# A two-layer graph network on one core: stores moved behind loads, GpSimd's order changed, part of V's split moved to GpSimd

## The chip, the cores and the metric

One NeuronCore of a Trainium2 chip runs the whole program. The metric is device time in microseconds of that core; each kernel was run several times, and the median is the number that counts. A separate profiled execution gives the trace.

## What is computed

64 graphs of 256 nodes with 512 features each go through two layers. `x` is (64, 256, 512), `adj` is (64, 256, 256), all float32.

```python
# layer 0
h = relu(layernorm(x))
q, k, v = h @ Wq.T + bq, h @ Wk.T + bk, h @ Wv.T + bv
weight = adj * exp(q @ k.T)
x = x + (weight / weight.sum(axis=2)) @ v
# layer 1
h = relu(layernorm(x))
A_hat = adj + eye
d = A_hat.sum(-1) ** -0.5
x = x + (A_hat * d[:, None] * d[None, :]) @ (h @ W + b)
```

## The kernel before

Every matrix product is done in float32 accuracy with three passes over "high" and "low" parts: a tile X is split into X_hi (rounded, written mostly by ScalarE, ACT) and X_lo = X - X_hi (a subtraction on VectorE, DVE, or GpSimd, POOL). TensorE (PE) then multiplies hi by hi, hi by lo and lo by hi (`product`, L1158, L1160 and L1161). Two products are done by a scheme with seven block products instead of eight: V = h Wv (`values`, blocks V1 to V7), and Y = Z W of layer 1 (`part`, R1 to R7). The sums that the scheme needs are `ht_sum` (POOL, L338 to L343) and `z_sum` (DVE, L858 to L869).

The program is a software pipeline over graphs: `steps` calls `step(this, ...)` for each graph, as a loop over 3 to 62 and with separate steps at either end. One step does layer 0 of graph `this`, layer 1 of graph `this - 1`, and prepares graphs `this + 1` and `this + 2`. There is no planner. Each engine has its own `step` with its order written out by hand, and semaphores are all that ties engines together. An engine works its list strictly in order, so a waiting instruction holds back all behind it.

What follows is one step in the order in which PE walks it, with the helpers of the other engines that matter below.

- **G** = M applied to ht (48 matmuls): ACT's `g_high` (L513) and DVE's `g_low` (L764) split it, for j = 0 and j = 1.
- **V** (42 matmuls): V1, V6, V5, V4, V2, V7, V3. V6 wants both halves of `ht_sum_lo` (POOL L349). V2 wants `v_p1` (ACT `keep_p1`, L498). V7 wants `v_u2` (DVE `value_u2`, L773).
- **Z** of the graph before (24 matmuls): wants `h1_lo` (DVE L883) and `hat_lo` (POOL L368).
- **S**, the attention logits (24 matmuls), then R1, and R2 behind `z_lo[1]` (DVE L862), then R4 and R5 behind the exponentials `e` (ACT L660).
- **O** = P V (24 matmuls), which wants all of `v_lo` and `p_lo`, with R6 between its halves, then R7 and R3.

The scale of layer 1's normalization runs through three engines: DVE computes `neg_mean_1` (L937), ACT the squares (L544), DVE `ve_1` (L1028), POOL the power `rs_1` (L406), DVE `sc_1` and `nb_1` (L1033, L1035, semaphore `ln_1_ready`), then ACT writes `h1` and `h1_hi` (L598, L600), and DVE `h1_low` (L883) and `add_bias` (L878, into x1b).

DVE's `turn_dn` (L849) waits for POOL's `row_norms` (L323, L325). `transpose_adjacency` (L841) overwrites `adjt` and so waits for POOL's `hat_low` (L368), which reads it. `sums_of_l` (L944 twice, then L949) comes between `z_low_first` and `z_low_second` (L862).

V's split has three pieces: `v_hi[0]`, `v_hi[1]`, `v_hi[2]` on ACT (L616, L625, L652), and their low parts on DVE: `value_low` (L794), `value_low_upper` (L801) and `value_low_lower` (L806, 128x512). POOL computes ht_sums, rs_x (L319), z_sum_lo (L393) and ht_lo (L455) in this order at the end of its step, and at the start diagonal_ones (L361), ht_sums_low (L349 twice), row_norms, rs_1, hat_low, x_with_bias (L330, twice).

All loads and stores go through SyncE's one queue (SP), issued in this order in a step: h to a scratch in DRAM (L259), the two stores of y behind `y_ready` (L265), adj_in (L269), the four loads of h_blocks (L205), xb (L249), x_in (L243), the two small stores of dn (L284), dn_row (L288), adj_blocks (L199).

Of the kernel before, what the change touches and what calls it, by code (L numbers as in the profile page):

```python
# [12 lines left out]
def gnn_program(nc, x, adj, wq, bq, wk, bk, wv, bv, w, b, out):  # L13
# [19 lines left out]
    with ctx:  # L33
# [57 lines left out]
        with nc.sbuf_tensor("v", [P, NT, 2, HD + 2], fp32) as v:  # L91
# [79 lines left out]
        vk_ready = sems("vk_ready")  # L171
        g_done, g_hi_ready, g_lo_ready = sems("g_done"), sems("g_hi_ready"), sems("g_lo_ready")
        v_done, v_hi_ready, v_lo_ready = sems("v_done", 7), sems("v_hi_ready", 3), sems("v_lo_ready", 3)
        v_p1_ready, v_p5_ready, v_u2_ready, v_u3_ready = (
            sem("v_p1_ready"), sem("v_p5_ready"), sem("v_u2_ready"), sem("v_u3_ready"))
        v12_ready, v21_ready, v22_ready = sem("v12_ready"), sem("v21_ready"), sem("v22_ready")
# [49 lines left out]
        @block.sync  # L226
        def _(sp):
            for o in range(DC):
                sp.dma_start(wk_in[:, o, :], wk[o * P:(o + 1) * P, :]).then_inc(wqk_loaded[o], 16)
            sp.dma_start(x_in[:], x[0].rearrange("(t p) d -> p t d", p=P)).then_inc(x_loaded, 16)  # L230
            sp.dma_start(wv_in[:], wv.rearrange("(c p) d -> p c d", p=P)).then_inc(wv_loaded, 16)
            sp.dma_start(adj_in[:], adj[0].rearrange("(t p) n -> p t n", p=P)).then_inc(adj_loaded, 16)
            sp.dma_start(xb[:], x[0].rearrange("(t p) d -> p t d", p=P)).then_inc(xb_loaded, 16)
            load_blocks(sp, adj.rearrange("g n m -> (g n m)")[0:N * N])
            for block, (i, j) in zip((B11, T3, B21, B22), ((0, 0), (0, 1), (1, 0), (1, 1))):
                sp.dma_start(w_parts[:, block], w.rearrange("(i c p) (j d) -> i j p c d", i=2, c=2, j=2)[i, j]).then_inc(
                    w_loaded, 16)

            adj_flat, x_flat = adj.rearrange("g n m -> (g n m)"), x.rearrange("g n d -> (g n d)")

            def load_x(this):
                x_second = x_flat[bass.ds(sp.snap((this + 1) * (N * D)), N * D)]
                sp.dma_start(x_in[:], x_second.rearrange("(t p d) -> p t d", p=P, d=D)).then_inc(x_loaded, 16)  # L243

            def load_xb(this):
                x_this = x_flat[bass.ds(sp.snap((this - 1) * (N * D)), N * D)]
                sp.wait_ge(x1_ready[0], this - 1)
                sp.wait_ge(x1_ready[1], this - 1)
                sp.dma_start(xb[:], x_this.rearrange("(t p d) -> p t d", p=P, d=D)).then_inc(xb_loaded, 16)  # L249

            def step(this, prev, main, ahead, older=True, second=True):
                if prev and not older:
                    load_xb(this)
                if prev and ahead:
                    sp.wait_ge(h_ready[0], this + 1)
                    sp.wait_ge(h_ready[1], this + 1)
                    if older:
                        sp.wait_ge(h_blocks_loaded, (this - 2) * (16 * P // 32))
                    sp.dma_start(h_dram.rearrange("(t p) d -> p t d", p=P), h[:]).then_inc(h_stored, 16)  # L259
                    if not older:  # L260
                        load_x(this)
                if prev and older:
                    for t in range(NT):
                        sp.wait_ge(y_ready[t], this - 2)
                        sp.dma_start(out[this - 3, t * P:(t + 1) * P, :], y[:, t, :]).then_inc(stored, 16)  # L265
                if main and ahead:
                    adj_next = adj_flat[bass.ds(sp.snap(this * (N * N)), N * N)]
                    sp.wait_ge(rsum_ready, this)
                    sp.dma_start(adj_in[:], adj_next.rearrange("(t p n) -> p t n", p=P, n=N)).then_inc(adj_loaded, 16)  # L269
                if prev and ahead:  # L270
                    sp.wait_ge(h_stored, (this - 1) * 16)
                    if older:
                        sp.wait_ge(ht_ready[1], this)
                    load_h_blocks(sp)
                if main and prev and older:
                    load_xb(this)
                if second and prev and older:
                    load_x(this)
                if main:
                    sp.wait_ge(dn_turned_ready, this)  # L280
                    if prev:
                        sp.wait_ge(dn_row_loaded, (this - 1) * 16)
                    for t in range(NT):
                        sp.dma_start(dn_dram[t], dn_turned[t::32, :]).then_inc(dn_stored, 16)  # L284
                    sp.wait_ge(dn_stored, this * (16 * NT))
                    if prev:
                        sp.wait_ge(s_sum_ready, this - 1)
                    sp.dma_start(dn_row[:], dn_dram.rearrange("t q c -> (t q c)").partition_broadcast(P)).then_inc(  # L288
                        dn_row_loaded, 16)
                if main and ahead:  # L290
                    sp.wait_ge(adjt_ready, this)
                    load_blocks(sp, adj_next)
                if second and not prev:
                    sp.wait_ge(h_ready[0], this + 1)
                    sp.wait_ge(h_ready[1], this + 1)
                    load_x(this)

            steps(sp, step)
            for t, a, ready, value in ((0, 0, y11_ready, B), (0, 1, y_ready[0], B), (1, 0, y_ready[1], B),
                                       (1, 1, y_ready[1], B + 1)):  # L300
                sp.wait_ge(ready, value)
                cols = slice(a * HD, (a + 1) * HD)
                sp.dma_start(out[B - 1, t * P:(t + 1) * P, cols], y[:, t, cols]).then_inc(stored, 16)
            sp.wait_ge(stored, B * 16 * NT + 16 * NT)

        @block.gpsimd
        def _(pool):
# [80 lines left out]

            def z_sums_low_second(graph, this=None):
                if this is not None:  # L390
                    pool.wait_ge(v_lo_ready[2], this)
                pool.wait_ge(z_sum_hi_ready, 2 * graph)
                pool.tensor_tensor(z_sum_lo[:, S3:S4 + 1], z_sum[:, S3:S4 + 1], z_sum_hi[:, S3:S4 + 1].bitcast(fp32),  # L393
                                   ALU.subtract).then_inc(z_sum_lo_by_pool, 1)

            def step(this, prev, main, ahead, older=True, second=True):
                if prev and older:

                    diagonal_ones(this - 1)
                    if main:  # L400
                        ht_sums_low(this)
                        pool.wait_ge(d_ready, this - 1)
                        pool.wait_ge(dn_turned_ready, this - 1)
                        row_norms(this)
                        pool.wait_ge(ve_1_done, this - 1)
                        pool.tensor_tensor(rs_1[:], ve_1[:], minus_half[:], ALU.pow).then_inc(rs_1_done, 1)  # L406
                    hat_low(this - 1, older)
                if prev and not older:
                    ht_sums_low_half(this, 0)
# [35 lines left out]
                if main and ahead:  # L445
                    pool.wait_ge(v_done[V3], this)
                    ht_sums(this + 1)
                if second and main and (older or not prev):
                    x_power(this + 2)
                if main and prev and older:  # L450
# [11 lines left out]
        def _(act):  # L462
# [113 lines left out]
            def step(this, prev, main, ahead, older=True, second=True):  # L576
# [12 lines left out]
                    x1_squares(this)  # L589
                if main and not prev:  # L590
                    act.wait_ge(u_ready, 1)
                if main and (not prev or older):
                    g_high(0, this)
                if prev:

                    for t in range(NT):
# [4 lines left out]
                                       bias=nb_1[:, t:t + 1]).then_inc(h1_ready[t], 1)  # L601
                        if main and not older and t == 0:
                            keep_p1(this)
                if main:
                    if not prev or older:
                        keep_p1(this)
# [81 lines left out]
        def _(dve):  # L688
# [287 lines left out]
            def step(this, prev, main, ahead, older=True, second=True):  # L976
# [45 lines left out]
                if prev and main and older:  # L1022
# [5 lines left out]
                    dve.tensor_scalar(ve_1[:], x1_square[:], 1.0 / D, EPS, ALU.mult, ALU.add).then_inc(ve_1_done, 1)  # L1028
                    dve.wait_ge(d_ready, this - 1)
                    dve.wait_ge(neg_mean_1_ready, this - 2)  # L1030
                    turn_dn(this, prev)
                    dve.wait_ge(rs_1_done, this - 1)
                    dve.tensor_tensor(sc_1[:], rs_1[:], d[:], ALU.mult).then_inc(sc_1_done, 1)  # L1033
                    dve.wait_ge(sc_1_done, this - 1)
                    dve.tensor_tensor(nb_1[:], neg_mean_1[:], sc_1[:], ALU.mult).then_inc(ln_1_ready, 1)  # L1035
                    transpose_adjacency(this, prev)
                    g_low(0, this)
                    h1_low(0, this - 1)
                    add_bias(0, this - 1)
                    value_u2(this)  # L1040
                    h1_low(1, this - 1)
                if main and not prev:
                    value_u2(this)
                    x_variance(this + 1)
# [45 lines left out]
                if main:  # L1090
# [11 lines left out]
                    p_low(this)  # L1102
                    if prev and older:
                        value_low_upper(this)
                        value_low_lower(this)
                        if second:
                            x_shift(this + 2)
                    if prev and not older:
# [43 lines left out]
        def _(pe):  # L1152
# [173 lines left out]
            def step(this, prev, main, ahead, older=True, second=True):  # L1326
# [61 lines left out]
                if main:  # L1388

                    pe.wait_ge(p_lo_ready[1], this)  # L1390
                    if not prev:
                        pe.wait_ge(consts_ready, 2)
                    for lower_part in v_lo_ready:
                        pe.wait_ge(lower_part, this)
                    pe.wait_ge(v12_ready, this)
                    pe.wait_ge(v21_ready, this)
                    pe.wait_ge(vk_ready[1], this)
# [39 lines left out]
```

## Time and profile before

| | us |
|---|---|
| median of 3 runs | 1873.71 |
| lowest, highest | 1871.33, 1873.95 |
| the profiled execution, its own time | 1872.89 |
| its span, first to last instruction | 1871.1 |

Busy shares of the span: PE 90%, DVE 85%, ACT 66%, POOL 57%; the granted TensorE clock averages 0.974 of full speed, and the DMA engines are busy 44% of the time on the main queue. A step of the loop takes some 28 us. A row of a timeline reads: start in us, duration in us, engine, line, operation, output<-inputs, shapes, count, and in brackets how long the engine had been idle before it and what released it. Consecutive DVE or ACT instructions overlap by some 0.07 us in such rows, since the records hold the start and the end of an instruction that is pipelined with the next.

### The profile page before, as it was taken

How to read it: one execution, taken by the hardware profiler on the slowest of the kernel's cores; microseconds unless marked ns; L12 is line 12 of the kernel's file. 1: busy time of each engine (PE TensorE's matmuls, PEld its weight loads, DVE VectorE, ACT ScalarE, POOL GpSimd, SP SyncE). 2: the span in 40 equal slices, each digit the busy share in tenths (PEclk: the TensorE clock that was granted, in tenths of full speed). 3: DMA queues.
4: the chain of work that ended last, by engine and by line, in shares of the span. 5: the costliest groups of instructions: out<-in, count | busy, mean ns of one | idle time of the engine just before them, and what ended most of it. 6: DMA issues, size and time to landing. Idle time of an engine off the chain costs nothing. (4 is left out here: it accounts for less than half of the span.)

```text
span 1871.1 us, 42042 instructions
## 1 busy us (share of the span) xinstructions
PE 1677.5 (90%) x13201; PEld 1623.8 (87%) x13201; DVE 1590.6 (85%) x3894; ACT 1240.0 (66%) x2890; POOL 1058.6 (57%) x1165
## 2 busy tenths in 40 slices
PE   8799899898898898999998988988988988988987
PEld 7788889898898898888888988988988988988987
DVE  7888888888888888888888888888888888888887
ACT  5566666766766666676676666666666666666663
POOL 4555655565556456556555555555555555564562
PEclk9899998999999999999999999999999999999998
DMA  5344353454453443543544544544544544534421
GB/s 172 84 117 125 96 129 104 111 133 107 107 131 104 114 126 95 129 117 104 129 111 110 129 110 112 129 111 111 129 108 113 128 107 105 133 101 117 132 69 48
DMA packets 495265, 212.68 MB, mean 114 GB/s; under 512 B 402576, under 2 KB 428688, under 8 KB 495248
## 3 DMA queue, kind: packets, MB, share of 16 engines
q1 hardware_dynamic: 493328, 210.89, 44.4%
q10 hardware_dynamic: 1920, 1.58, 0.3%
q8 instruction: 9, 0.15, 0.0%
q14 instruction: 8, 0.07, 0.0%
HBM read 146.28 MB, written 66.13 MB: 114 GB/s over the span
## 5 line engine op out<-in xcount | busy, mean ns | idle before, releaser
L330 POOL TENSOR_TENSOR xb<-xb,bv_row 128x512 f32<-128x512 f32 x128 | 163.7, 1300 | 406.5 <-DMA xb<-in_x_dram 392.6
L1158 PE MATMUL ps<-ht_hi,m_hi 128*128 128x256 f32 x1024 | 286.2, 279 | 2.8 <-issue 2.7
L1160 PE MATMUL ps<-ht_lo,m_hi 128*128 128x256 f32 x1024 | 288.4, 282 | 0.0
L1161 PE MATMUL ps<-ht_hi,m_lo 128*128 128x256 f32 x1024 | 287.5, 281 | 0.0
L1158 PE MATMUL ps<-w_hi,z_hi 128*128 128x256 f32 x384 | 125.4, 327 | 115.4 <-DVE z_lo L862 59.3
L898 DVE SCALAR_TENSOR_TENSOR late<-ps,d,late 128x256 f32<-128x256 f32 x504 | 219.5, 476 | 4.5 <-PE ps L1161 2.1
L1158 PE MATMUL ps<-v_hi,p_hi 128*128 128x258 f32 (+1 forms) x512 | 155.7, 304 | 64.1 <-DVE v_lo L801 54.6
L1158 PEld LDWEIGHTS ps<-w_hi,z_hi 128*128 128x128 f32 x384 | 75.1, 195 | 141.3 <-DVE z_lo L862 72.5
L1158 PEld LDWEIGHTS ps<-ht_hi,m_hi 128*128 128x128 f32 x1024 | 193.4, 189 | 3.2 <-issue 2.9
L529 ACT ACTIVATE unused_x<-x_in 128x512 f32<-128x512 f32 x128 | 79.7, 624 | 172.5 <-DMA x_in<-in_x_dram 172.5
L1161 PEld LDWEIGHTS ps<-ht_hi,m_lo 128*128 128x128 f32 x1024 | 193.5, 189 | 0.0
L1160 PEld LDWEIGHTS ps<-ht_lo,m_hi 128*128 128x128 f32 x1024 | 193.2, 189 | 0.0
L393 POOL TENSOR_TENSOR z_sum_lo<-z_sum,z_sum_hi 128x512 fp32r<-128x512 f32 x64 | 82.6, 1290 | 172.1 <-DVE v_lo L806 156.0
L1158 PEld LDWEIGHTS ps<-v_hi,p_hi 128*128 128x128 f32 x512 | 101.8, 199 | 76.5 <-issue 70.2
L349 POOL TENSOR_TENSOR ht_sum_lo<-ht_sum,ht_sum_hi 128x512 fp32r<-128x512 f32 x128 | 164.2, 1305 | 2.5 <-ACT ht_sum_hi L508 2.5
L598 ACT ACTIVATE late<-late,nb,sc 128x512 f32<-128x512 f32 x128 | 103.6, 809 | 89.5 <-DVE nb L1035 86.2
L455 POOL TENSOR_TENSOR ht_lo<-ht,ht_hi 128x512 fp32r<-128x512 f32 x124 | 158.3, 1300 | 0.0
L1158 PE MATMUL ps<-w_hi,z_sum_hi 128*128 128x256 f32 x512 | 149.9, 293 | 5.6 <-DVE late L898 4.9
L319 POOL TENSOR_TENSOR rs_x<-ve_x,minus_half 128x2 f32<-128x2 f32 x64 | 51.3, 801 | 180.4 <-DVE ve_x L815 180.4
L1160 PE MATMUL ps<-w_lo,z_sum_hi 128*128 128x256 f32 x512 | 149.3, 292 | 0.0
L1160 PE MATMUL ps<-v_lo,p_hi 128*128 128x258 f32 (+1 forms) x512 | 149.2, 291 | 0.0
L1161 PE MATMUL ps<-w_hi,z_sum_lo 128*128 128x256 f32 x512 | 148.8, 291 | 0.0
(195 smaller groups left out, 7051.9 us busy)
## 6 DMA issues: line engine op xcount, KB each, us to landing
x_in<-in_x_dram SPq DMA_DIRECT2D x64, 512.0 KB, 4.9
xb<-in_x_dram SPq DMA_DIRECT2D x64, 512.0 KB, 4.4
out_dram<-late SPq DMA_DIRECT2D x126, 256.0 KB, 2.2
h_scratch<-h SPq DMA_DIRECT2D x62, 512.0 KB, 2.8
h_blocks<-h_scratch SPq DMA_DIRECT2D x248, 128.0 KB, 3.9
adj_in<-in_adj_dram SPq DMA_DIRECT2D x64, 256.0 KB, 3.1
adj_blocks<-in_adj_dram SPq DMA_DIRECT2D x256, 64.0 KB, 2.5
dn_row<-dn_scratch SPq DMA_DIRECT2D x64, 128.0 KB, 2.9
```

Of the source, the lines that this page charges most:

```text
L319: pool.tensor_tensor(rs_x[:], ve_x[:], minus_half[:], ALU.pow).then_inc(rs_x_done, 1)
L330: last = pool.tensor_tensor(xb[:, t, :], xb[:, t, :], bv_row[:], ALU.add)
L349: pool.tensor_tensor(ht_sum_lo[:, pair], ht_sum[:, pair], ht_sum_hi[:, pair].bitcast(fp32), ALU.subtract).then_inc(ht_sum_lo_ready, 1)
L393: pool.tensor_tensor(z_sum_lo[:, S3:S4 + 1], z_sum[:, S3:S4 + 1], z_sum_hi[:, S3:S4 + 1].bitcast(fp32), ALU.subtract).then_inc(z_sum_lo_by ...
L455: pool.tensor_tensor(ht_lo[:, 2 * j:2 * j + 2, :], ht[:, 2 * j:2 * j + 2, :], ht_hi[:, 2 * j:2 * j + 2, :].bitcast(fp32), ALU.subtract).th ...
L529: last = act.activation(unused_x[:, t, :], x_in[:, t, :], ACT.Copy, accum_out=x_sum[:, t:t + 1])
L598: act.activation(h1[:, t, :], x1[:, t, :], ACT.Relu, scale=sc_1[:, t:t + 1], bias=nb_1[:, t:t + 1])
L898: return dve.scalar_tensor_tensor(y[:, t, cols], ps[:, bank, 0:HD], scale[:, t:t + 1], base[:, t, cols], ALU.mult, ALU.add)
L1158: pe.matmul(dst, a_hi[:, c, cols], b_hi[:, c, :], start=(first and c == 0), stop=False, skip_group_check=not first)
L1160: pe.matmul(dst, a_hi[:, c, cols], b_lo[:, c, :], start=False, stop=False, skip_group_check=not first)
L1161: end = pe.matmul(dst, a_lo[:, c, cols], b_hi[:, c, :], start=False, stop=(c == chunks - 1), skip_group_check=not first)
```

## The change

Five things are done.

- SyncE issues the two stores of y behind the loads of xb and x_in instead of ahead of adj_in.
- GpSimd writes only the first half of ht_sum_lo before rs_1, then waits for `ln_1_ready` (a wait that no data asks for), and then writes the second half and does row_norms.
- GpSimd writes the low part of V's lower rows (128x512) behind ht_sums, under a semaphore of its own, and its z_sum_lo waits for v_lo_ready[1] in place of v_lo_ready[2]. VectorE no longer does value_low_lower in the loop's steps.
- ScalarE writes h1 and h1_hi for both halves ahead of g_high(0).
- VectorE does h1_low(0) and add_bias(0) directly after nb_1, then turn_dn, transpose_adjacency, h1_low(1), g_low(0) and value_u2.

```diff
@@ -171,6 +171,7 @@
         vk_ready = sems("vk_ready")
         g_done, g_hi_ready, g_lo_ready = sems("g_done"), sems("g_hi_ready"), sems("g_lo_ready")
         v_done, v_hi_ready, v_lo_ready = sems("v_done", 7), sems("v_hi_ready", 3), sems("v_lo_ready", 3)
+        v_lo_by_pool = sem("v_lo_by_pool")
         v_p1_ready, v_p5_ready, v_u2_ready, v_u3_ready = (
             sem("v_p1_ready"), sem("v_p5_ready"), sem("v_u2_ready"), sem("v_u3_ready"))
         v12_ready, v21_ready, v22_ready = sem("v12_ready"), sem("v21_ready"), sem("v22_ready")
@@ -259,10 +260,6 @@
                     sp.dma_start(h_dram.rearrange("(t p) d -> p t d", p=P), h[:]).then_inc(h_stored, 16)
                     if not older:
                         load_x(this)
-                if prev and older:
-                    for t in range(NT):
-                        sp.wait_ge(y_ready[t], this - 2)
-                        sp.dma_start(out[this - 3, t * P:(t + 1) * P, :], y[:, t, :]).then_inc(stored, 16)
                 if main and ahead:
                     adj_next = adj_flat[bass.ds(sp.snap(this * (N * N)), N * N)]
                     sp.wait_ge(rsum_ready, this)
@@ -276,6 +273,10 @@
                     load_xb(this)
                 if second and prev and older:
                     load_x(this)
+                if prev and older:
+                    for t in range(NT):
+                        sp.wait_ge(y_ready[t], this - 2)
+                        sp.dma_start(out[this - 3, t * P:(t + 1) * P, :], y[:, t, :]).then_inc(stored, 16)
                 if main:
                     sp.wait_ge(dn_turned_ready, this)
                     if prev:
@@ -388,7 +389,7 @@
 
             def z_sums_low_second(graph, this=None):
                 if this is not None:
-                    pool.wait_ge(v_lo_ready[2], this)
+                    pool.wait_ge(v_lo_ready[1], this)
                 pool.wait_ge(z_sum_hi_ready, 2 * graph)
                 pool.tensor_tensor(z_sum_lo[:, S3:S4 + 1], z_sum[:, S3:S4 + 1], z_sum_hi[:, S3:S4 + 1].bitcast(fp32),
                                    ALU.subtract).then_inc(z_sum_lo_by_pool, 1)
@@ -398,12 +399,14 @@
 
                     diagonal_ones(this - 1)
                     if main:
-                        ht_sums_low(this)
+                        ht_sums_low_half(this, 0)
+                        pool.wait_ge(ve_1_done, this - 1)
+                        pool.tensor_tensor(rs_1[:], ve_1[:], minus_half[:], ALU.pow).then_inc(rs_1_done, 1)
+                        pool.wait_ge(ln_1_ready, this - 1)
+                        ht_sums_low_half(this, 1)
                         pool.wait_ge(d_ready, this - 1)
                         pool.wait_ge(dn_turned_ready, this - 1)
                         row_norms(this)
-                        pool.wait_ge(ve_1_done, this - 1)
-                        pool.tensor_tensor(rs_1[:], ve_1[:], minus_half[:], ALU.pow).then_inc(rs_1_done, 1)
                     hat_low(this - 1, older)
                 if prev and not older:
                     ht_sums_low_half(this, 0)
@@ -445,6 +448,10 @@
                 if main and ahead:
                     pool.wait_ge(v_done[V3], this)
                     ht_sums(this + 1)
+                if main and prev and older:
+                    pool.wait_ge(v_hi_ready[2], this)
+                    pool.tensor_tensor(v_lo[:, 1, :, 0:HD], v[:, 1, :, 0:HD], v_hi[:, 1, :, 0:HD].bitcast(fp32),
+                                       ALU.subtract).then_inc(v_lo_by_pool, 1)
                 if second and main and (older or not prev):
                     x_power(this + 2)
                 if main and prev and older:
@@ -589,7 +596,7 @@
                     x1_squares(this)
                 if main and not prev:
                     act.wait_ge(u_ready, 1)
-                if main and (not prev or older):
+                if main and not prev:
                     g_high(0, this)
                 if prev:
 
@@ -601,6 +608,8 @@
                                        bias=nb_1[:, t:t + 1]).then_inc(h1_ready[t], 1)
                         if main and not older and t == 0:
                             keep_p1(this)
+                    if main and older:
+                        g_high(0, this)
                 if main:
                     if not prev or older:
                         keep_p1(this)
@@ -1028,17 +1037,17 @@
                     dve.tensor_scalar(ve_1[:], x1_square[:], 1.0 / D, EPS, ALU.mult, ALU.add).then_inc(ve_1_done, 1)
                     dve.wait_ge(d_ready, this - 1)
                     dve.wait_ge(neg_mean_1_ready, this - 2)
-                    turn_dn(this, prev)
                     dve.wait_ge(rs_1_done, this - 1)
                     dve.tensor_tensor(sc_1[:], rs_1[:], d[:], ALU.mult).then_inc(sc_1_done, 1)
                     dve.wait_ge(sc_1_done, this - 1)
                     dve.tensor_tensor(nb_1[:], neg_mean_1[:], sc_1[:], ALU.mult).then_inc(ln_1_ready, 1)
-                    transpose_adjacency(this, prev)
-                    g_low(0, this)
                     h1_low(0, this - 1)
                     add_bias(0, this - 1)
+                    turn_dn(this, prev)
+                    transpose_adjacency(this, prev)
+                    h1_low(1, this - 1)
+                    g_low(0, this)
                     value_u2(this)
-                    h1_low(1, this - 1)
                 if main and not prev:
                     value_u2(this)
                     x_variance(this + 1)
@@ -1102,7 +1111,6 @@
                     p_low(this)
                     if prev and older:
                         value_low_upper(this)
-                        value_low_lower(this)
                         if second:
                             x_shift(this + 2)
                     if prev and not older:
@@ -1390,8 +1398,12 @@
                     pe.wait_ge(p_lo_ready[1], this)
                     if not prev:
                         pe.wait_ge(consts_ready, 2)
-                    for lower_part in v_lo_ready:
-                        pe.wait_ge(lower_part, this)
+                    pe.wait_ge(v_lo_ready[0], this)
+                    pe.wait_ge(v_lo_ready[1], this)
+                    if prev and older:
+                        pe.wait_ge(v_lo_by_pool, this - 2)
+                    else:
+                        pe.wait_ge(v_lo_ready[2], this)
                     pe.wait_ge(v12_ready, this)
                     pe.wait_ge(v21_ready, this)
                     pe.wait_ge(vk_ready[1], this)
```

## Rows read from the trace of the kernel before

**Rows 1.** The waits of the whole trace: engine, line waited for, total us, times, longest

```profile
POOL xb L330 <- DMA xb<-in_x_dram: 392.6, 60, 7.7
PE ps L1158 <- DVE z_lo L862: 59.3, 59, 1.8
```

**Rows 2.** Timeline of VectorE in one step of the loop, up to the scale

```profile
1191.45 0.42 DVE L801 TENSOR_TENSOR v_lo<-v,v_hi 128x256 fp32r<-128x256 f32 x1
1191.79 0.69 DVE L806 TENSOR_TENSOR v_lo<-v,v_hi 128x512 fp32r<-128x512 f32 x1
...
1196.66 0.17 DVE L927 RECIPROCAL rinv<-ps 128x1 f32<-128x1 f32 x1 [0.70 <-PE ps L1161]
...
1197.72 0.82 DVE L937 TENSOR_SCALAR neg_mean<-x_sum 128x2 f32<-128x2 f32 x1
...
1200.13 0.17 DVE L1028 TENSOR_SCALAR ve<-x_square 128x2 f32<-128x2 f32 x1
...
1201.75 1.25 DVE L1033 TENSOR_TENSOR sc<-rs,d 128x2 f32<-128x2 f32 x1 [0.25 <-POOL rs L406]
1203.03 0.16 DVE L1035 TENSOR_TENSOR nb<-neg_mean,sc 128x2 f32<-128x2 f32 x1
```

**Rows 3.** The same timeline, from transpose_adjacency to the next step's L801

```profile
1203.22 0.71 DVE L841 STREAM_TRANSPOSE adjt<-adj_blocks 128x512 f32<-128x512 f32 x1
...
1206.54 0.43 DVE L773 TENSOR_TENSOR v_u<-ps,v_p 128x258 f32<-128x258 f32 x1 [0.40 <-ACT v_p L498]
1206.88 0.68 DVE L883 TENSOR_TENSOR h_lo<-late,h_hi 128x512 fp32r<-128x512 f32 x1
1207.48 0.74 DVE L878 SCALAR_TENSOR_TENSOR late<-b_row,sd,late 128x512 f32<-128x512 f32 x1
1208.14 0.87 DVE L764 SCALAR_TENSOR_TENSOR g_lo<-ps,u_col,g_hi 128x256 fp32r<-128x256 f32 x2
...
1212.53 0.24 DVE L811 TENSOR_SCALAR neg_mean<-x_sum 128x2 f32<-128x2 f32 x1
...
1214.35 0.95 DVE L944 CUSTOM_DVE_ANT_0 unused_a<-adj_kept,dn_row,dn_wide 128x256 f32<-128x256 f32 x1
...
1215.42 0.68 DVE L862 TENSOR_TENSOR z_lo<-ps,z_hi 128x512 fp32r<-128x512 f32 x1
...
1219.52 0.42 DVE L801 TENSOR_TENSOR v_lo<-v,v_hi 128x256 fp32r<-128x256 f32 x1
```

**Rows 4.** Timeline of GpSimd in the same step

```profile
1197.22 2.56 POOL L349 TENSOR_TENSOR ht_sum_lo<-ht_sum,ht_sum_hi 128x512 fp32r<-128x512 f32 x2
...
1201.02 0.69 POOL L406 TENSOR_TENSOR rs<-ve,minus_half 128x2 f32<-128x2 f32 x1
1201.67 1.30 POOL L368 TENSOR_TENSOR hat_lo<-adjt,hat_hi 128x512 fp32r<-128x512 f32 x1
1209.31 2.55 POOL L330 TENSOR_TENSOR xb<-xb,bv_row 128x512 f32<-128x512 f32 x2 [6.33 <-DMA xb<-in_x_dram]
...
1214.21 0.81 POOL L343 TENSOR_TENSOR ht_sum<-ht,ht_sum 128x256 f32<-128x256 f32 x1
```

**Rows 5.** Timelines of ScalarE, SyncE's queue and TensorE in the same step

```profile
1203.95 0.80 ACT L600 ACTIVATE h_hi<-late,nb,sc 128x512 fp32r<-128x512 f32 x1
...
1214.00 0.62 ACT L652 ACTIVATE v_hi<-v 128x512 fp32r<-128x512 f32 x1
...
1205.03 0.44 SPq L249 DMA_DIRECT2D xb<-in_x_dram  x1
...
1192.79 0.36 PE L1158 MATMUL ps<-v_hi,p_hi 128*128 128x258 f32 x1 [1.22 <-DVE v_lo L801]
...
1207.31 0.28 PE L1158 MATMUL ps<-wt_hi,ht_sum_hi 128*128 128x256 f32 x1
```

**Rows 6.** L944 and L1035 in the whole trace: ns min/median/max, first and last start

```profile
L944 DVE CUSTOM_DVE_ANT_0 unused_a<-adj_kept,dn_row,dn_wide x128: 470/918/1504, 50.5 to 1836.1; 128x256 f32<-128x256 f32 x128
...
L1035 DVE TENSOR_TENSOR nb<-neg_mean,sc x62: 160/161/164, 96.8 to 1826.6; 128x2 f32<-128x2 f32 x62
```

## The prediction

> **What bounds the kernel now.** I read the waits first, then one step of the loop on each engine. TensorE looks like the bound at 90% busy, but its waits end on VectorE: it waits for z_lo once in nearly every step [rows 1]. The longest wait of the trace is GpSimd's for xb, 6.54 us a step (392.6 over 60) [rows 1]. That wait is the first thing to follow, since the stores of y stand ahead of that load.
>
> I take the step that starts with L801 at 1191.45 and count from there; the next L801 comes at 1219.52, so it is 28.07 long [rows 2, 3]. VectorE is nearly always at work in it, and four of its instructions are longer than their size explains. L1033 handles 128x2 elements in 1.25 us where L1035, of the same kind and size, takes 0.16. It ends at 1203.00, just after GpSimd's hat_low ends (1202.97) [rows 2, 4]. L937, also 128x2, takes 0.82 and ends when the first half of L349 must be ending [rows 2, 4]. The second L944 takes 0.95 where the shortest takes 0.47, and it ends 0.28 after GpSimd's L343 (1215.02) [rows 3, 4, 6]. So certain VectorE instructions stand still until GpSimd's running instruction is over. Those seen here read two tiles in SBUF, or are tiny ones. The transposes and the reads of PSUM show nothing of it.
>
> This makes the late xb load costly although GpSimd is only 57% busy: load, x_with_bias, ht_sums, then the second L944, then z_lo, then TensorE. L343's end is 5.71 behind L330's start, and L862 starts 0.40 behind that [rows 3, 4].
>
> The Trainium skill (SBUF, "Who interferes with whom") states this as a lock: a VectorE instruction with two SBUF inputs contends with a GpSimd instruction that reads SBUF, and whichever is first holds the pair to its end. L1033 agrees with 1.25 against 0.16 [rows 2].
>
> **Part 1, the stores behind the loads.** This removes SyncE's wait for y from in front of adj_in, h_blocks, xb and x_in. xb was issued at 1205.03 and used at 1209.31 [rows 4, 5]. Without the wait the order is free to go as soon as h has been stored, some us earlier, so GpSimd will wait for the other condition of x_with_bias, the end of add_bias(1) on VectorE, which in this step would be 1208.22 (L878 starts at 1207.48 and lasts 0.74) [rows 3]. GpSimd could start 1.05 earlier. The stores themselves cost nothing where they land: y is not overwritten until the next step's R1. The dn stores come behind them on the queue, but no longer behind the x loads' data.
>
> **Part 2, value_low_lower to GpSimd.** VectorE loses L806, 0.69 [rows 2]. TensorE's O started at 1.34, 0.31 after L806's end at 1.03 [rows 2, 5]. Now it can start some 0.37 after L801's end at 0.42 (one more wait to pass, 0.06 as an estimate), so 0.79: **0.55 gained**. All that follows O moves: the second L927 from 5.21 to 4.66. GpSimd's z_sum_lo, and with it everything up to the first half of ht_sum_lo, comes 0.61 earlier (L801's end instead of L806's).
>
> **Part 3, around the scale.** L937 ended at 7.09 with the first half of L349; 0.61 earlier is 6.48. The squares and ve_1 follow at the same distance: ve_1 ends at 8.24 instead of 8.85 [rows 2]. GpSimd is idle then, so rs_1 (0.69) runs at once, to 8.96, and then waits, which leaves L1033 free: 0.16. With L1035's 0.16 and 0.04 between each, nb is done at 9.36. It was 11.74: **2.4 us earlier** [rows 2, 4].
>
> But VectorE's next work is now h1_low(0), which waits for ScalarE's h1 and h1_hi. L600 ended 1.56 after nb's end (1204.75 against 1203.19) [rows 2, 5], so h1_low(0) starts at 10.95. Before, transpose_adjacency and g_low(0) covered this. Here VectorE stands idle for 1.6 us. From the starts in rows 3, h1_low takes 0.60 to the next instruction and add_bias 0.66. They end at 12.2. Meanwhile GpSimd, released at 9.4, does half of L349 (1.28), row_norms (about 0.9) and hat_low (1.30): 12.9 at best. Its row_norms and hat_low read SBUF, as h1_low and add_bias do, and meet them between 10.95 and 12.2. At worst hat_low starts only at 12.25 and ends at 13.55. I take the worst, since both VectorE instructions read two SBUF tiles and stand back to back. transpose_adjacency waits for hat_low: 13.58. Then 0.64 for it (as between 1203.22 and g_low at 1203.86), h1_low(1) 0.60, g_low(0) 0.79, value_u2 0.34, add_bias(1) 0.66. g_low(1) starts at **16.61; it was 16.69** [rows 3]. So the 2.4 us are given back almost whole, to waits for ScalarE and GpSimd. Bounds: 15.9 if hat_low isn't delayed, 17.3 if row_norms is pushed behind add_bias(0) and hat_low comes yet 0.65 later.
>
> value_u2 ends at 16.05. TensorE, 0.55 earlier than before, would reach V7 at 15.3 (15.86 less 0.55 [rows 5]) and waits 0.75. That is covered: with 60 matmuls of 0.12 from V7 to the end of S and six more for R1, it reaches R2 near 24.0, while z_lo (below) comes later. If z_lo came at 23.3 the cover would be gone, and it would cost up to 0.1.
>
> **Part 4, what the shorter wait for xb buys.** GpSimd starts x_with_bias at 16.75 (it was 17.86) and by the same 5.71 ends ht_sums at 22.46. On VectorE, L811 came 4.39 after g_low(1), of which 0.28 was L790 standing behind GpSimd; I take 4.11, so 20.72, with its end at 21.0. The first L944 follows 0.77 later, at 21.8, when L343 has just begun (21.65). It stands until 22.4, the second one takes 0.47 more: both are done at 23.1.
>
> **Part 5, the new instruction on GpSimd.** v_lo's lower rows wait for ScalarE's L652. That ended 1.85 after L811's end (1214.62 against 1212.77) [rows 3, 5]: now 22.85. So GpSimd is ready with its 1.3 us instruction (L368 has the same size, 1.30 [rows 4]) at 22.9, and gets its turn when the second L944 is over, near 23.05. VectorE's next is sd (L949), 128x2, from two SBUF tiles, ready at 23.15: 0.2 too late. It would stand as L1033 did, until 24.3. L862 starts at **24.35; it was 23.97**. The instruction that left VectorE (0.69) comes back as a wait of up to 1.2, at the place on which TensorE waits.
>
> The Trainium skill (Perfetto Trace Analysis, "Optimizing Scalar/DVE Operations") warns that moving work between VectorE and GpSimd might not help because of their common read port. By that alone the 0.55 of part 2 would be returned; the sum above goes by the rows.
>
> **The sum.** From L862 to the next L801 was 4.10 and is unchanged: the step is 28.45. The average step before was 28.36 (L1035's first and last start, 61 steps [rows 6]), longer than the one shown by 0.29: 0.21 by a later xb (6.54 against 6.33), which goes away, and 0.08 by disturbed steps, which stay. So 28.53 against 28.36, 0.17 more, times 62 steps: +10.5. On the profiled execution's 1872.89 that is 1883.4. The median of the runs is 0.8 higher: **1884 us**.
>
> **The rivals.**
>
> A. sd slips in ahead of v_lo. Then L862 starts at 23.25, the step is 27.43 on average, 0.93 less, 62 times: -58, **1816 us**. Against it: my 0.2 us margin. For it: that margin is the difference of two sums of six terms, each good to 0.1. It decides at L944's end: if ht_sums ends 0.3 earlier relative to VectorE, or ScalarE's L652 comes 0.25 later, sd is first. Since GpSimd no longer waits for a transfer, all steps should fall the same way. Chance 0.32.
>
> B. The waits behind h1 are longer: row_norms and hat_low queue behind VectorE's pair and g_low(1) starts at 17.3. That is 0.7 on top of the forecast: +43, **1927 us**. Chance 0.07.
>
> C. The forecast's mechanism, sized differently. 0.3 us a step is 19 us. With g_low(1) at 16.3 the result is 1865. The chance of the case is 0.61, of which 0.16 fall below, 0.11 within and 0.34 above the bounds of 0.2% that a measurement of this kernel can tell from no change.
>
> D. The change doesn't do what it says: xb stays late, because the queue is held by the store of h rather than by y. Then L862 can't come before the old 23.97. Included in C, as it gives no more than that.
>
> **How the numbers follow.** Faster: 0.32 of A and 0.16 of C, 0.48. Same: 0.11. Slower: 0.34 and 0.07, 0.41. The forecast is 1884, its own range 1862 to 1902. Faster and slower both hold much, so the whole range takes in A with an error of 10 us: 1806 to 1902, leaving out B and the tails.
>
> **What would show it.** GpSimd's wait for xb should be released by add_bias (L878), not by the DMA. L1033 should take 0.16. VectorE should show a new idle time of 1.6 us before h1_low(0), released by h_hi, and one before transpose_adjacency, released by hat_lo. TensorE should wait for v_u before V7. L949 decides: a median near 1.2 us is the forecast, 0.16 is rival A. If L944 takes 0.47 both times, my timing of ht_sums against VectorE is wrong, and the time will lie below 1816.

## The result

The changed kernel is slower by 0.3%: a median of 1879.03 us (1877.07 to 1880.03, 7 runs) against 1873.71 us (7 runs), a ratio of 1.0031 with a 95% interval of 1.0018 to 1.0044. Its profiled execution has a span of 1877.3 us.

VectorE's busy time fell from 1590.6 us to 1502.2, by 88 us, GpSimd's rose from 1058.6 to 1176.3, and the whole got 5 us longer. The lines of the page of the changed kernel (first the busy times, and from the chain of work that ended last its shares by engine):

```profile
PE 1680.4 (90%) x13201; PEld 1623.4 (86%) x13201; DVE 1502.2 (80%) x3832; ACT 1231.7 (66%) x2890; POOL 1176.3 (63%) x1227
...
DVE 36%; POOL 32%; issue 22%; ACT 5%; PE 1%; DVEq 1%; POOLq 1%; SPq 1%; DMA 0%; ACTq 0%
```

The waits of the changed kernel answer to [rows 1]. The 392.6 us behind the DMA are gone, and GpSimd waits for add_bias (L887 is the old L878). TensorE has a new wait for value_u2 (L782), and VectorE has three: for h1_hi, for hat_lo, and a longer one for rs.

```profile
POOL xb L331 <- DVE late L887: 205.4, 62, 3.3
...
DVE h_lo L892 <- ACT h_hi L607: 100.2, 63, 1.6
...
DVE adjt L850 <- POOL hat_lo L369: 63.3, 62, 1.1
...
DVE sc L1041 <- POOL rs L404: 56.5, 62, 0.9
...
PE ps L1166 <- DVE v_u L782: 51.9, 62, 1.1
PE ps L1166 <- DVE z_lo L871: 46.7, 61, 0.8
```

One step of the changed kernel on VectorE, from L810 (the old L801) at 1167.48 to the next at 1195.94. It is 28.46 us long, and every time below is to be read less 1167.48 against [rows 2, 3]. The last row is of the next step and answers to L1033:

```profile
1178.61 0.69 DVE L892 TENSOR_TENSOR h_lo<-late,h_hi 128x512 fp32r<-128x512 f32 x1 [1.59 <-ACT h_hi L607]
...
1181.20 0.71 DVE L850 STREAM_TRANSPOSE adjt<-adj_blocks 128x512 f32<-128x512 f32 x1 [1.01 <-POOL hat_lo L369]
...
1184.18 0.87 DVE L773 SCALAR_TENSOR_TENSOR g_lo<-ps,u_col,g_hi 128x256 fp32r<-128x256 f32 x2
...
1189.33 1.02 DVE L953 CUSTOM_DVE_ANT_0 unused_a<-adj_kept,dn_row,dn_wide 128x256 f32<-128x256 f32 x1
...
1190.28 0.48 DVE L953 CUSTOM_DVE_ANT_0 unused_a<-adj_kept,dn_row,dn_wide 128x256 f32<-128x256 f32 x1
...
1190.80 1.13 DVE L958 TENSOR_TENSOR sd<-s_sum,dn_wide 128x2 f32<-128x2 f32 x1
1191.85 0.68 DVE L871 TENSOR_TENSOR z_lo<-ps,z_hi 128x512 fp32r<-128x512 f32 x1
...
1195.94 0.42 DVE L810 TENSOR_TENSOR v_lo<-v,v_hi 128x256 fp32r<-128x256 f32 x1
...
1205.11 0.16 DVE L1041 TENSOR_TENSOR sc<-rs,d 128x2 f32<-128x2 f32 x1 [0.91 <-POOL rs L404]
```

GpSimd in the same step, answering to [rows 4]:

```profile
1178.63 1.22 POOL L326 TENSOR_TENSOR dn_wide<-rsum,minus_half 128x2 f32<-128x2 f32 x1
1179.81 1.30 POOL L369 TENSOR_TENSOR hat_lo<-adjt,hat_hi 128x512 fp32r<-128x512 f32 x1
1184.43 2.54 POOL L331 TENSOR_TENSOR xb<-xb,bv_row 128x512 f32<-128x512 f32 x2 [3.32 <-DVE late L887]
...
1189.32 0.74 POOL L344 TENSOR_TENSOR ht_sum<-ht,ht_sum 128x256 f32<-128x256 f32 x1
1190.51 1.40 POOL L453 TENSOR_TENSOR v_lo<-v,v_hi 128x512 fp32r<-128x512 f32 x1 [0.44 <-ACT v_hi L661]
```

L453 starts at 1190.51, L958 at 1190.80. L453 ends at 1191.91, L958 at 1191.93, with 1.13 us for 256 numbers that take 0.16 elsewhere. Then L871 starts, on which TensorE waits. The collision is in nearly every step, as the line of L958 over the whole trace shows (ns min/median/max):

```profile
L958 DVE TENSOR_TENSOR sd<-s_sum,dn_wide x64: 160/1130/1133, 52.5 to 1843.7; 128x2 f32<-128x2 f32 x64
...
L1043 DVE TENSOR_TENSOR nb<-neg_mean,sc x62: 160/161/164, 95.3 to 1831.4; 128x2 f32<-128x2 f32 x62
```

L1043 gives the average step: (1831.4 - 95.3) / 61 = 28.46, against 28.36 before. From one start of L1043 to the next, all 61 steps lie between 28.44 and 28.60 us. In the kernel before they lie between 27.46 and 30.38 (starts of L1035).

The granted clock is a rival for the cause, since its mean is only 0.976 here. In 17 places of the loop, from 455 us on in every third step, TensorE runs at half clock (1.2 GHz instead of 2.4) for some 3.4 us. Such a stretch and one without, one step on (length, busy us, then the granted clock, DMA share and GB/s):

```profile
1222.50:1226.50 4.00, 3.65 (x18) 0.59 0.00 0
1251.00:1255.00 4.00, 3.19 (x24) 1.00 0.00 0
```

The first two steps that hold such a stretch take 28.60 and 28.51 us, and the 15 later ones are as long as the steps without, so the half clock costs the changed kernel next to nothing.

### The profile page after: what moved, and what is told of

It reads as the page before. It is cut to its first block, busy times and chain, and to the rows that moved or that the text cites. A ratio compares the mean times of both kernels' runs of the same rounds, so it can differ in the third digit from the quotient of the medians.

```text
span 1877.3 us, 42042 instructions
## 1 busy us (share of the span) xinstructions
PE 1680.4 (90%) x13201; PEld 1623.4 (86%) x13201; DVE 1502.2 (80%) x3832; ACT 1231.7 (66%) x2890; POOL 1176.3 (63%) x1227
## 4 chain that ended last, share of the span: by engine, by line
DVE 36%; POOL 32%; issue 22%; ACT 5%; PE 1%; DVEq 1%; POOLq 1%; SPq 1%; DMA 0%; ACTq 0%
POOL ht_sum_lo L350 8%; POOL ht_lo L462 8%; DVE g_lo L773 5%; DVE unused_a L953 4%; POOL hat_lo L369 4%; DVE ht L841 4%; POOL dn_wide L326 4%; POOL adjt L362 3%; POOL rs L404 2%; DVE z_lo L871 2%; DVE late L887 2%; ACT z_sum_hi L577 2%; ACT e L669 1%; DVE z_sum L876 1%; DVE p_lo L982 1%
## 5 line engine op out<-in xcount | busy, mean ns | idle before, releaser
L1166 PE MATMUL ps<-wt_hi,ht_sum_hi 128*128 128x256 f32 (+1 forms) x512 | 151.1, 295 | 52.5 <-DVE v_u L782 51.9
L892 DVE TENSOR_TENSOR h_lo<-late,h_hi 128x512 fp32r<-128x512 f32 x128 | 85.9, 671 | 100.2 <-ACT h_hi L607 100.2
L634 ACT ACTIVATE v_hi<-v 128x256 fp32r<-128x256 f32 x64 | 26.8, 419 | 199.1 <-DVE v L797 199.1
L577 ACT ACTIVATE z_sum_hi<-z_sum 128x512 fp32r<-128x512 f32 x128 | 79.9, 625 | 116.3 <-DVE z_sum L876 116.3
L1166 PEld LDWEIGHTS ps<-wt_hi,ht_sum_hi 128*128 128x128 f32 x512 | 96.2, 188 | 65.7 <-DVE v_u L782 64.8
```

Source lines behind the costliest of these rows:

```text
L577: act.activation(z_sum_hi[:, pair], z_sum[:, pair], ACT.Copy).then_inc(z_sum_hi_ready, 1)
L892: dve.tensor_tensor(h1_lo[:, t, :], h1[:, t, :], h1_hi[:, t, :].bitcast(fp32), ALU.subtract).then_inc(h1_lo_ready[t], 1)
L1166: pe.matmul(dst, a_hi[:, c, cols], b_hi[:, c, :], start=(first and c == 0), stop=False, skip_group_check=not first)
```

## The experiments

The theory under test: VectorE's instructions with two SBUF inputs stand behind a running GpSimd instruction, so what counts is when GpSimd's instructions fall against them, not how busy either engine is. The rivals: the step is set by VectorE's busy time, by TensorE's new wait, or by none of these. All ratios are to the kernel before on the same chip. Those chips differ by up to 0.5% in the kernel before (1873.71 us for the result, 1865.25 and 1872.02 in the two groups of runs below), so ratios are compared, not times. Where no row is shown, the time at which something starts in a step is the median over the kernel's steps, counted from the start of L801 or the line that answers to it.

| kernel | parts in it | us | ratio, 95% interval |
|---|---|---|---|
| p1_stores | stores behind loads | 1820.26 | 0.9760 (0.9737 to 0.9783) |
| p2_vlow | V's lower rows on GpSimd | 1886.77 | 1.0128 (1.0095 to 1.0161) |
| p3_scale | order around the scale | 1866.20 | 0.9996 (0.9979 to 1.0013) |
| e1_sd_first | all three, sd kept ahead | 1819.68 | 0.9753 (0.9729 to 0.9777) |
| p1_p2 | first two | 1849.94 | 0.9881 (0.9862 to 0.9901) |
| p1_p3 | first and third | 1858.04 | 0.9927 (0.9908 to 0.9946) |
| p1_p2_sd | first two, sd kept ahead | 1782.14 | 0.9525 (0.9506 to 0.9544) |
| p1_p2_sd_scale2 | the same and another order of the scale | 1720.99 | 0.9195 (0.9176 to 0.9214) |

### sd kept ahead of GpSimd's new instruction

```diff
                 if main and prev and older:
                     pool.wait_ge(v_hi_ready[2], this)
+                    pool.wait_ge(sd_ready, this)
                     pool.tensor_tensor(v_lo[:, 1, :, 0:HD], ...
```

> The changed kernel with one wait more: GpSimd's low part of V's lower rows also waits for sd_ready, so that VectorE's sd (128x2) is always issued ahead of it. Theory one, sd stands behind GpSimd's 1.3 us instruction and that delays z_lo and TensorE: sd falls from a median of 1.13 us to 0.16, the second part of z_lo starts near 23.4 us after L810 instead of 24.4, the step falls from 28.46 to 27.5 us, 62 steps, and the time to some 1818 us. Theory two, the step is set elsewhere (by V7's wait for value_u2 on TensorE, or by VectorE's own new idle time): sd is short, another wait takes up most of the gain, and the time stays above 1860 us.

Measured: 0.9753. One more wait makes the changed kernel 2.8% faster (0.9753 / 1.0031 = 0.972). sd has a median of 160 ns:

```profile
L959 DVE TENSOR_TENSOR sd<-s_sum,dn_wide x64: 160/160/573, 53.3 to 1785.7; 128x2 f32<-128x2 f32 x64
...
L1044 DVE TENSOR_TENSOR nb<-neg_mean,sc x62: 160/161/164, 96.1 to 1773.4; 128x2 f32<-128x2 f32 x62
```

The step is (1773.4 - 96.1) / 61 = 27.50 us, as expected under theory one. TensorE still waits for value_u2, and for longer (66.0 us instead of 51.9), without holding the time at 1860. The stretches at half clock are gone from the loop too (the mean is 0.992), but they had cost nothing. That settles the cause: 0.96 us a step were lost to this one collision.

### The stores alone

```diff
-                if prev and older:
-                    (the two stores of y, behind y_ready)
                 if main and ahead:
 ...
                 if second and prev and older:
                     load_x(this)
+                if prev and older:
+                    (the two stores of y, behind y_ready)
```

> The kernel before with the stores of y moved behind the loads, and nothing else. Theory one, the late load of xb shifts GpSimd's sums against VectorE and so sets z_lo: x_with_bias starts with the end of add_bias instead of with the DMA, L862 starts at 23.4 after L801 instead of 24.0 to 24.1, and the time is 1873.7 less 62 times 0.8, some 1825 us. Theory two, GpSimd at 57% busy is off the path and the load is hidden anyway: the wait moves from the DMA to another releaser and the time stays within 5 us of 1873.7.

Measured: 0.9760, 1820.26 us. The stores moved behind the loads are worth 2.4% by themselves, although GpSimd is 58% busy and no VectorE instruction was removed. In a step that starts with L801 at 1130.31 (the next is at 1157.79, 27.48 later), the end of the two L944 no longer hangs on a late load:

```profile
1153.10 0.47 DVE L944 CUSTOM_DVE_ANT_0 unused_a<-adj_kept,dn_row,dn_wide 128x256 f32<-128x256 f32 x1
...
1153.62 0.16 DVE L949 TENSOR_TENSOR sd<-s_sum,dn_wide 128x2 f32<-128x2 f32 x1
1153.70 0.69 DVE L862 TENSOR_TENSOR z_lo<-ps,z_hi 128x512 fp32r<-128x512 f32 x1
...
1157.79 0.42 DVE L801 TENSOR_TENSOR v_lo<-v,v_hi 128x256 fp32r<-128x256 f32 x1
```

L862 is at 23.39. It was 23.97 in the step of [rows 3]. The average step falls by more, from 28.36 to 27.48, since that step was one of the shorter ones: with no load waited for, all steps take 27.47 to 27.50, the last two apart. TensorE's wait for it fell from 59.3 us [rows 1] to 14.6, and GpSimd's for xb is released by add_bias:

```profile
POOL xb L330 <- DVE late L878: 335.0, 62, 5.4
...
PE ps L1158 <- DVE z_lo L862: 14.6, 60, 0.3
```

### V's lower rows on GpSimd alone

The diff is the third bullet of the change with TensorE's wait for it: L806 leaves VectorE, the GpSimd instruction comes in behind ht_sums.

> The kernel before with the low part of V's lower rows moved to GpSimd, and nothing else. Theory one: O starts 0.55 us earlier, but GpSimd's new instruction stands directly behind the sums, is ready before sd and makes sd wait some 1.2 us; L862 starts near 24.6 after L801 instead of 24.0, the step is 0.5 to 0.7 us longer and the time some 1905 to 1915 us. Theory two, VectorE's busy time is what counts: 0.69 us off VectorE gives 0.55 us a step back, some 1840 us.

Measured: 1.0128. Moving 0.69 us of work off the busier engine makes the kernel 1.3% slower. VectorE's busy time didn't even fall in the trace (1601.2 us against 1590.6), since standing still counts as busy. sd's duration:

```profile
L954 DVE TENSOR_TENSOR sd<-s_sum,dn_wide x64: 163/1102/1249, 53.0 to 1847.7; 128x2 f32<-128x2 f32 x64
```

The mechanism is theory one's; the size was expected at 1905 to 1915 us, and it is 1887, on a chip where the kernel before takes 1865. So 22 us were lost where 31 to 41 were expected. The load of xb came earlier too, which the expectation left out: the stores of y are issued 0.59 us earlier in the step than in the kernel before, and x_with_bias starts at 17.24 instead of 18.04. That this is all of the difference isn't shown.

### The order around the scale alone

> The kernel before with the order around x1's scale alone (GpSimd, ScalarE and VectorE). Theory one: L1033 falls from 1.24 to 0.16 us, and the gain goes into a wait for h1_hi of 1.6 us and one for hat_lo of about 1 us on VectorE, so that g_low(1) starts 0.4 to 0.5 us later than before; the late xb hides that as GpSimd's sums are later still, and the time stays within 10 us of 1873.7. Theory two: the shorter scale is worth its 1.1 us a step, some 1806 us.

Measured: 0.9996. sc takes 0.16 us here instead of 1.24, and nothing comes of it, as theory one has it. g_low(1) starts at 17.30 instead of 16.69, and the second part of z_lo, still set by the late xb, at 24.06 instead of 24.16. VectorE waits 100.2 us for h1_hi and 63.7 us for hat_lo:

```profile
DVE h_lo L887 <- ACT h_hi L602: 100.2, 63, 1.6
...
DVE adjt L845 <- POOL hat_lo L368: 63.7, 62, 1.1
```

### Two parts at a time

The first expectation is for p1_p2, the second for p1_p3.

> The stores behind the loads and V's lower rows on GpSimd, with the scale's order as in the kernel before; so the changed kernel without its third part. By the port theory everything up to g_low(1) comes 0.55 to 0.6 us earlier than in p1_stores, and then sd stands 1.0 us behind GpSimd's new instruction: the step is 27.48 - 0.55 + 1.0 = 27.9 us, the time some 1846 us, between p1_stores (1820) and the changed kernel (1879). If the third part is free, as its own run suggests, this should equal the changed kernel.

> The stores behind the loads and the order around x1's scale, V's lower rows left on VectorE. Without the late xb the third part has no cover: g_low(1) starts 0.5 us later than in p1_stores, x_with_bias and the sums with it, and the second part of z_lo at 23.9 instead of 23.4; the step is 28.0 us and the time some 1852 us. If the third part costs nothing, it equals p1_stores at 1820 us.

Measured: 0.9881 (1850 us) and 0.9927 (1858 us), against 1846 and 1852 expected. The third part isn't free. Put on top of p1_stores it costs 1.7% (0.9927 / 0.9760), and on top of p1_p2 1.5% (1.0031 / 0.9881). Alone it cost nothing, because the late xb covered its delay. The first part takes that cover away: g_low(1) starts at 17.30 instead of 16.69 of p1_stores, and the second part of z_lo at 24.00 instead of 23.39. So the parts don't add: 0.9760, 1.0128 and 0.9996 multiply to 0.9881, and the changed kernel is at 1.0031.

p1_p2 has a second collision. 47 of its 61 steps take 27.66 to 27.87 us, but 10 take some 29.1. Each of those 10 has a stretch of TensorE at half clock around its start (0.57 in the first row, whose step starts at 1205.9). There neg_mean (L942) comes some 0.9 us late, when the second half of ht_sum_lo is running on GpSimd, and it stands until that ends at 1213.63:

```profile
1204.80:1208.80 4.00, 4.00 (x23) 0.57 0.00 0
...
1212.30 1.36 DVE L942 TENSOR_SCALAR neg_mean<-x_sum 128x2 f32<-128x2 f32 x1
...
1211.08 2.55 POOL L350 TENSOR_TENSOR ht_sum_lo<-ht_sum,ht_sum_hi 128x512 fp32r<-128x512 f32 x2
```

In 4 more steps such a stretch costs 0.1 us, as L942 comes just ahead of that half and takes 0.17 us. In the changed kernel the second half waits for ln_1_ready, and a late neg_mean takes 0.17 us and costs nothing. So the third part costs 0.6 us in an undisturbed step and spares these.

### The two useful parts without the collision

The diff is the first two parts with the wait for `sd_ready`.

> As p1_p2, with GpSimd's new instruction held until sd is done. The collision is gone and the 0.55 us of the shorter VectorE path should come out in full: step 26.9 us, some 1786 us, 34 us below p1_stores. If moving the work gives nothing even then, it stays at 1820 us.

Measured: 0.9525, 1782.14 us, with an average step of 26.89 us. V's lower rows on GpSimd are now worth 2.4% (0.9525 / 0.9760), where the same move cost 1.3% with the collision.

### Another order around the scale

Against p1_p2_sd:

```diff
                         pool.tensor_tensor(rs_1[:], ve_1[:], minus_half[:], ALU.pow).then_inc(rs_1_done, 1)
+                        pool.wait_ge(ln_1_ready, this - 1)
                     hat_low(this - 1, older)
 ...
-                    transpose_adjacency(this, prev)
                     g_low(0, this)
+                    transpose_adjacency(this, prev)
                     h1_low(0, this - 1)
```

> As p1_p2_sd, with another order around the scale: GpSimd does row_norms and rs_1 as in the kernel before and then waits for ln_1_ready ahead of hat_low, so that sc runs unblocked; VectorE does g_low(0) while it waits, then transpose_adjacency, h1_low(0), add_bias(0). sc saves 1.1 us, and g_low(0) and hat_low cover the wait for h1_hi. g_low(1) should start 1.2 us earlier than in p1_p2_sd; TensorE becomes the bound before all of it is realized, since its 204 matmuls of 0.12 us and two or three waits come to about 25.5 us: step 25.3 to 26.0 us, 1690 to 1735 us. If the scale is off the path, it stays at p1_p2_sd's time.

Measured: 0.9195, 1720.99 us, 8% faster than the kernel before. The wait for ln_1_ready is the third part's idea, put in front of hat_low alone; ScalarE's order is the old one, and g_low(0) fills all but 0.76 us of VectorE's time before transpose_adjacency, which starts 0.09 us behind the end of GpSimd's hat_low. sc and sd both take 0.16 us:

```profile
1157.41 0.16 DVE L1040 TENSOR_TENSOR sc<-rs,d 128x2 f32<-128x2 f32 x1 [0.25 <-POOL rs L407]
1159.32 0.71 DVE L848 STREAM_TRANSPOSE adjt<-adj_blocks 128x512 f32<-128x512 f32 x1 [0.76 <-issue]
...
1169.39 0.16 DVE L956 TENSOR_TENSOR sd<-s_sum,dn_wide 128x2 f32<-128x2 f32 x1
```

TensorE is busy 95% of the span, and the step is (1674.8 - 96.4) / 61 = 25.88 us, within the range expected, but not because TensorE became the bound. g_low(1) starts 1.02 us earlier than in p1_p2_sd (15.08 against 16.10) instead of 1.2, and the second part of z_lo (21.79 against 22.80) and the step follow it in full:

```profile
PE 1626.1 (95%) x13201; PEld 1591.5 (93%) x13201; DVE 1450.6 (84%) x3832; ACT 1236.9 (72%) x2890; POOL 1138.2 (66%) x1227
...
L1042 DVE TENSOR_TENSOR nb<-neg_mean,sc x62: 160/161/163, 96.4 to 1674.8; 128x2 f32<-128x2 f32 x62
```

## Why the prediction came out as it did

The forecast was 1884 us with 1806 to 1902, and the time is 1879. Its mechanism is the one that the traces show. The rise itself was forecast at 10.5 us and is 5.3, and a range of 96 us that takes in rival A's result too would have been met in either order of sd and v_lo.

- **What bounds the kernel.** Right: the late xb set GpSimd's sums, and these set z_lo. p1_stores shows it alone.
- **Part 2, 0.55 gained.** Right in kind, and larger: the second reciprocal (the old L927) comes at 4.50 in the changed kernel (1200.44 less 1195.94), 4.66 by the sum, so 0.71 was gained. The extra 0.16 went into neg_mean's stand behind GpSimd (0.97 us instead of 0.82).
- **Part 3.** Right. nb starts at 9.37 (1205.31) and is done at 9.53 (9.36 by the sum), h1_low(0) starts at 11.13 (10.95 by the sum) behind a wait of 1.59, transpose_adjacency at 13.72 (13.58), g_low(1) at 16.70 (16.61). The bound that I took for hat_low, 12.25, was nearly exact: it starts at 12.33. That is partly luck, since it came about another way. The sum had hat_low itself stand until add_bias(0) is over. But hat_low starts 0.15 before the end of add_bias(0) (1179.81 against 1179.96), directly behind L326, and it is L326 that was late: GpSimd's power of 256 numbers took 1.22 us instead of 0.70, h1_low(0) having started 0.02 ahead of it.
- **TensorE's wait for value_u2.** The right place, 1.12 us instead of 0.75. It was covered, as said: the changed kernel with sd kept ahead has it too and reaches 27.50 a step.
- **Part 4 and part 5.** Right, in the order that decided: GpSimd's instruction was 0.29 ahead of sd (1190.51 against 1190.80), 0.2 by the sum. z_lo's second part starts at 24.37, 24.35 by the sum. x_with_bias was 0.20 late against the sum (16.95), and the sums behind it took 0.08 less, so small errors of both signs stand behind that agreement.
- **The sum.** The step was to be 28.45 and is 28.46. The term that was mis-sized is the 0.08 us a step for disturbed steps, which I let stay. In the changed kernel the average step and the one shown are both 28.46. Without that term the sum gives 0.09 a step and +5.6 us; measured are +5.3. p1_stores shows that moving the stores alone takes these steps away: all of its steps are alike. Two things go with them in the kernel before. One is loads of xb that are later still: p3_scale has such loads and no stretch at half clock in its loop, and its steps lie between 28.01 and 29.16 us. The other is those stretches, which the five longest steps before (29.20 to 30.38 us) all hold. How the 0.08 is shared between the two isn't shown.
- **Rival A** was the nearest one. e1_sd_first brought it about: z_lo's second part at 23.40 (23.25 by the sum) and a step of 27.50 (27.43). The gain over the kernel before was given as 58 us and is 2.5%, some 46 us. In the step it is 28.36 less 27.50, 0.86 where 0.93 was given.
- **Rival B** didn't come. D didn't either: the load of xb is no longer waited for.
- **The chances** leaned to faster, 0.48 against 0.41, although the likeliest case was slower. The margin in the order of sd and v_lo was held to be less certain than it was. It rests on sums of durations that repeat within a few hundredths of a us in most steps of the changed kernel.

## What to carry to other kernels

Before moving work from VectorE to GpSimd, look for what VectorE does at the new place with two tiles from SBUF, however small: an instruction of 0.16 us can stand for the whole length of GpSimd's. A wait that no data asks for, on GpSimd, can be the cheapest repair, and here it turned a loss of 0.3% into a gain of 2.5%. Parts of a change are to be measured alone and in pairs: one that is free beside a late load can cost 1.5% once the load is in time, and a reordering that frees one instruction has to be paid with what it covered before.

## What the runs showed of the hardware

VectorE and GpSimd hold each other up in both directions. In the changed kernel GpSimd's L326 took 1.22 us instead of the 0.70 of its like in the kernel before (L325), where VectorE was idle, having started 0.02 us behind VectorE's h1_low. The Trainium skill (SBUF, "Who interferes with whom") says that issue order decides who blocks, and both L326 and L958 agree with it.

It isn't only instructions with two tiles from SBUF that stand. neg_mean (TENSOR_SCALAR, 128x2, one tile) took 0.97 us in the changed kernel and 1.36 in p1_p2's row above, where the shortest takes 0.17, and ended with GpSimd's ht_sum_lo. The profile shows such standing as busy time.

The granted clock of TensorE, mean over the span, was 0.974 before and 0.976 after, 0.970 in p2_vlow and 0.981 in p1_p2, and 0.992 to 0.995 in the six others. The four lower ones are those with stretches at half clock in the midst of the loop, and those in which TensorE waits most for the second part of z_lo: 46.7 to 98.1 us in all, against 14.9 at most in the others. What ties the two together was not tested. What a stretch costs depends on what stands behind it: next to nothing in the changed kernel, and 1.2 us in 10 steps of p1_p2.
